# Attention output computed transposed and normalised straight from PSUM, in an attention and mixture-of-experts kernel

## What is computed

```python
c = einsum('bsi,bij->bsj', x, cond_weight[ids]) + cond_bias[ids][:, None, :]
Q, K, V = lora_linear(c, ...).reshape(B, 64, 16, 16)          # one each
scores = einsum('bqhd,bkhd->bhqk', Q, K) / 4 + slopes * (k - q)
attn = softmax(scores, axis=-1)
out = einsum('bhqk,bkhd->bqhd', attn, V).reshape(B, 64, 256)
out = lora_linear(out, Wo, bo, Ao, Bo)
x = x + (c + rezero * out)
```

## Time and profile before

| | |
|---|---|
| runs | 883.76, 883.92, 885.71 us, median 883.92 |
| profiled execution | 885.9 us, of which the span from first to last instruction is 884.0 |
| PE busy, PEld busy | 828.5 us (94%), 689.5 us (78%) |
| DVE, ACT, POOL busy | 543.3 us (61%), 294.2 us (33%), 402.7 us (46%) |
| mean granted clock of PE | 0.986 |

### The profile page before, as it was taken

One profiled execution on the slowest core, in us unless ns is written; L12 is line 12 of the kernel. 1 busy time (PEld: TensorE's weight loads), 2 busy tenths in 40 slices (PEclk: granted clock), 3 DMA queues, 4 the chain that ended last, 5 costly groups with the idle time before them and its releaser, 6 DMA issues.

```text
span 884.0 us, 28455 instructions
## 1 busy us (share of the span) xinstructions
PE 828.5 (94%) x9821; PEld 689.5 (78%) x9822; DVE 543.3 (61%) x1231; ACT 294.2 (33%) x783; POOL 402.7 (46%) x511
## 2 busy tenths in 40 slices
PE   6899999999999999979999799999999999999995
PEld 5777777777777778856777588888888888888884
DVE  3675565556555556758887356666666666666662
ACT  0233323333333333334323223343333333333330
POOL 2133343334334444210100357676777676767662
PEclk7999999999999999999999899999999999999998
DMA  8445555454454443104862313232323232323222
GB/s 274 139 118 153 163 163 161 143 147 147 151 159 134 140 149 106 46 1 138 250 231 71 118 25 37 35 37 32 36 33 37 32 37 32 37 31 37 32 35 24
DMA packets 49004, 85.60 MB, mean 97 GB/s; under 512 B 7266, under 2 KB 27554, under 8 KB 48834
## 3 DMA queue, kind: packets, MB, share of 16 engines
q1 hardware_dynamic: 33634, 68.76, 25.2%
q0 software_dynamic: 13888, 15.13, 13.2%
q10 hardware_dynamic: 1440, 1.16, 0.5%
HBM read 68.48 MB, written 16.55 MB: 96 GB/s over the span
## 4 chain that ended last, share of the span: by engine, by line
PE 76%; POOL 8%; issue 6%; DVE 5%; ACT 2%; ACTq 1%; DMA 1%; POOLq 1%; another core or an unknown queue 0%; DVEq 0%
PE ps L1409 22%; PE ps L1397 13%; PE ps L1310 6%; PE ps L1113 5%; PE ps L1392 4%; PE ps L1188 3%; PE ps L1299 3%; PE ps L1132 3%; PE ps L1380 2%; PE ps L1160 2%; PE ps L1172 2%; PE ps L1203 2%; PE ps L1100 2%; PE ps L1219 1%; POOL be_bc L407 1%
## 5 line engine op out<-in xcount | busy, mean ns | idle before, releaser
L1409 PE MATMUL ps<-arena,stage 128*128 x900 | 206.6, 379 | 0.0
L1409 PEld LDWEIGHTS ps<-arena,stage 128*128 128x128 f32 x900 | 165.2, 190 | 19.5
L476 POOL DMA_INDIRECT out_dram<-stage,to_row x75 | 120.6, 1608 | 89.8 <-DVE stage L1030 85.2
L634 ACT ACTIVATE stage<-ps 128x384 f32<-128x384 f32 x150 | 71.3, 490 | 232.6 <-PE ps L1397 229.8
L1397 PE MATMUL ps<-token_rows,token_rows_T 64*128 64x128 f32 x1800 | 144.6, 289 | 0.0
L1397 PEld LDWEIGHTS ps<-token_rows,token_rows_T 64*128 64x128 f32 x1800 | 120.7, 191 | 0.0
L468 POOL DMA_INDIRECT token_rows<-gated_rows,from_row x75 | 75.1, 1001 | 76.6 <-DVE to_row L918 54.0
L1008 DVE COPY token_rows<-ps 128x128 f32<-128x128 f32 x75 | 21.9, 291 | 131.1 <-PE ps L1381 131.1
L386 POOL TENSOR_TENSOR arena<-arena 128x256 f32<-128x256 f32 x32 | 23.3, 728 | 172.6 <-DVE arena L759 172.5
L1015 DVE TENSOR_TENSOR stage<-ps,stage 128x384 f32<-128x384 f32 x150 | 75.9, 546 | 2.0 <-ACT stage L634 2.0
L1113 PE MATMUL ps<-arena 128*128 128x128 f32 x512 | 67.4, 286 | 5.5 <-ACT arena L529 5.5
(11 more groups left out here) (170 smaller groups left out, 1482.6 us busy)
## 6 DMA issues: line engine op xcount, KB each, us to landing
stage<-in_we_dram SPq DMA_DIRECT2D x36, 512.0 KB, 4.3
arena<-in_cond_w_dram SPq DMA_DIRECT2D x64, 256.0 KB, 2.9
arena<-in_we_dram SPq DMA_DIRECT2D x12, 768.0 KB, 4.8
arena<-in_x_both_dram SPq DMA_DIRECT2D x32, 256.0 KB, 2.6
arena<-in_L_cond_bias_dram SPq DMA_DIRECT2D x64, 64.0 KB, 2.8
out_dram<-arena SPq DMA_DIRECT2D x32, 128.0 KB, 1.7
be_bc<-in_be_rows_dram SPq DMA_DIRECT2D x13, 192.0 KB, 2.8
gated_rows<-token_rows POOLq DMA_DIRECT2D x2, 1152.0 KB, 10.3
```

The costliest lines, as they stand in the source:

```text
L476: pool.indirect_dma_start(out_rows, bass.IndirectOffsetOnAxis(to_row[:, t:t + 1], 0), y_sb[t % YR], None, compute_op=ALU.add).then_inc(d_a ...
L634: nc.scalar.activation(g_sb[hf], ps[:, 2 + hf, 0:HH], ACT.Gelu).then_inc(g_ok, 1)
L1409: last = mm(ps[:, 4 + s % 2, 0:D], actT_sb[s % 2][:, hf, j * P:(j + 1) * P], arena[:, ds(e * E2 + (NJ * hf + j) * D, D)], start=(hf == 0 a ...
```

## The change

The output is computed transposed. The stationary operand is now `vD`, 128 partitions by 32 columns (V of two heads, block-diagonal, without the columns of ones), and the moving one is the block of `probsT`, 64 columns. The result has 32 features of two heads on the partitions and 64 queries in the columns; g selects the 32 partitions, m and b the columns, so that the 16 products fill columns 0 to 255 of bank 7 with the output in the layout that `oT` has. Beside each stands a second product with the constant `head_ones` (128x32, ones in the rows of a head for its 16 columns), which gives that head's row sums, repeated over its 16 partitions, in columns 256 to 511 of bank 7. `normalize` takes the reciprocal of all 256 columns of sums and multiplies, and its result is `oT` itself. `o_transpose` and `oT_copy` are gone, and so are the four DVE copies of ones into `vD` at the start. In `merge_b` the new `attend` runs between the two halves of the merge (after L1219, ahead of L1223); in steps without a merge it comes after `condition`, as the last work of the step. `score`, with its wait for `o_sb(i-1)`, is untouched.

```diff
-        vD = [cut(2, 8, 34) for _ in range(2)]
+        vD = [cut(2, 8, 2 * HD) for _ in range(2)]
...
-        onorm = cut(D)
+        inverse = cut(D)
...
-            def oT_copy(i):
-                act.wait_ge(oT_ps, i + 1)
-                copy(oT, ps[:, 7, 0:D].rearrange("p (c n) -> p c n", c=KC)).then_inc(oT_sb, 1)
...
-            for s in range(2):
-                for h in range(2):
-                    V.tensor_copy(vD[s][:, :, :, 32 + h],
-                                  col["kv"][:, h:h + 1].unsqueeze(2).to_broadcast([P, 2, 8]))
...
             def normalize(i):
                 dve.wait_ge(o_ps, i + 1)
-                V.reciprocal(rsum.rearrange("p (a h) -> p a h", h=2), o_acc[:, :, 32:34]).then_inc(rsum_sb, 1)
-                dve.wait_ge(rsum_sb, i + 1)
-                V.tensor_tensor(onorm.rearrange("p (a h d) -> p a h d", h=2, d=HD),
-                                o_acc[:, :, 0:32].rearrange("p a (h d) -> p a h d", h=2),
-                                rsum.rearrange("p (a h) -> p a h", h=2).unsqueeze(3).to_broadcast([P, 8, 2, HD]),
+                if not isinstance(i, int) or i > 0:
+                    dve.wait_ge(att_ps, i)
+                V.reciprocal(inverse, ps[:, 7, D:2 * D]).then_inc(inverse_sb, 1)
+                dve.wait_ge(inverse_sb, i + 1)
+                V.tensor_tensor(oT.rearrange("p c n -> p (c n)"), ps[:, 7, 0:D], inverse,
                                 ALU.mult).then_inc(o_sb, 1)
...
-                for g in range(4):
-                    for m in range(KC):
-                        hp = 4 * m + g
-                        for b in range(2):
-                            last = mm(ps[b * S:(b + 1) * S, 2, hp * 34:(hp + 1) * 34],
-                                      probsT[:, 2 * g + m, b * S:(b + 1) * S], vD[int(odd)][:, b, hp, :],
-                                      start=True, stop=True)
-                last.then_inc(o_ps, 1)
-
-            def o_transpose(i):
-                pe.wait_ge(o_sb, i + 1)
                 if not isinstance(i, int) or i > 0:
                     pe.wait_ge(x2T_sb, i)
-                for c in range(KC):
-                    last = tr(ps[:, 7, c * P:(c + 1) * P], onorm[:, c * P:(c + 1) * P], ident)
-                last.then_inc(oT_ps, 1)
+                for m in range(KC):
+                    for b in range(2):
+                        for g in range(4):
+                            r, at = slice(32 * g, 32 * g + 32), m * P + b * S
+                            p = probsT[:, 2 * g + m, b * S:(b + 1) * S]
+                            mm(ps[r, 7, at:at + S], vD[int(odd)][:, b, 4 * m + g, :], p, start=True, stop=True)
+                            last = mm(ps[r, 7, D + at:D + at + S], col["head_ones"], p, start=True, stop=True)
+                last.then_inc(o_ps, 1)
 
             def output(i):
-                pe.wait_ge(oT_sb, i + 1)
+                pe.wait_ge(o_sb, i + 1)
...
-            def merge(n, j, arrived, rows):
+            def merge(n, j, arrived, rows, inside=lambda: None):
...
                            stage_w[j][:, c, 2 * g:2 * g + 2, :], start=(c == 0), stop=(c == KC - 1))
+                inside()
...
-                if not isinstance(i, int) or i > 0:
-                    o_transpose(i - 1)
...
-                attend(i, odd)
                 if two_more:
                     condition(i + 2, odd)
                 if merge_b:
-                    merge(*merge_b, rows=i - 1 if late else None)
+                    merge(*merge_b, rows=i - 1 if late else None, inside=lambda: attend(i, odd))
+                else:
+                    attend(i, odd)
```

More of the change, by code:

```diff
@@ L34 @@
 NEG = -3.0e38
-CONST_COLS = dict(ident=P, tri=P, kmask=2, kv=2, count_down=NE, tile_start=NT, slot_tile=NS,
+CONST_COLS = dict(ident=P, tri=P, kmask=2, count_down=NE, tile_start=NT, slot_tile=NS,
                   block=NLANG * NE, past_high=1, past_mid=1, lang_row=1, one_row=1,
-                  in_tile=P, part_back=1, pad_row=1, id_high=2 * PAIRS, half=2)
+                  head_ones=2 * HD, in_tile=P, part_back=1, pad_row=1, id_high=2 * PAIRS, half=2)
 SMALL_COLS = dict(wr_raw=KC * NE, bq=KC, bk=KC, rz=1, wr=NE)
@@ L135, in adaln_attn_moe @@
         smax = cut(H)
-        rsum = cut(H)
         wm = [cut(KC, D) for _ in range(4)]
@@ L223, in adaln_attn_moe @@
         (c_ps, c_ok, cT_ps, cT_sb, xbo_sb, xres_sb, q_ps, q_sb, k_ps, v_ps, k_sb, v_sb, s_ps, max_sb, shift_sb,
-         prob_sb, pT_ps, pTa_sb, pTv_sb, o_ps, rsum_sb, o_sb, oT_ps, oT_sb, att_ps, x2_sb, x2T_ps, x2T_sb,
+         prob_sb, pT_ps, pTa_sb, pTv_sb, o_ps, inverse_sb, o_sb, att_ps, x2_sb, x2T_ps, x2T_sb,
          t_ps, t_sb, tT_ps, tT_sb, lg_sb, kept_t, kept_x2) = [sem(n) for n in (
              "c_ps c_ok cT_ps cT_sb xbo_sb xres_sb q_ps q_sb k_ps v_ps k_sb v_sb s_ps max_sb shift_sb "
-             "prob_sb pT_ps pTa_sb pTv_sb o_ps rsum_sb o_sb oT_ps oT_sb att_ps x2_sb x2T_ps x2T_sb "
+             "prob_sb pT_ps pTa_sb pTv_sb o_ps inverse_sb o_sb att_ps x2_sb x2T_ps x2T_sb "
              "t_ps t_sb tT_ps tT_sb lg_sb kept_t kept_x2").split()]
@@ L565, in tile_steps @@
                     cT_copy(i + 1)
-                if not isinstance(i, int) or i > 0:
-                    oT_copy(i - 1)
                 if merge_a:
@@ L602, in _ @@
                 unit_copy(u, u)
-            oT_copy(NT - 1)
             tT_copy(NT - 2)
@@ L740, in pT_copy @@
                 V.tensor_copy(probsT[:, 4:8, :].rearrange("p a n -> p (a n)"), ps[:, 1, :]).then_inc(pTv_sb, 1)
-            o_acc = ps[:, 2, 0:8 * 34].rearrange("p (a n) -> p a n", n=34)
             def normalize(i):
                 dve.wait_ge(o_ps, i + 1)
-                V.reciprocal(rsum.rearrange("p (a h) -> p a h", h=2), o_acc[:, :, 32:34]).then_inc(rsum_sb, 1)
-                dve.wait_ge(rsum_sb, i + 1)
-                V.tensor_tensor(onorm.rearrange("p (a h d) -> p a h d", h=2, d=HD),
-                                o_acc[:, :, 0:32].rearrange("p a (h d) -> p a h d", h=2),
-                                rsum.rearrange("p (a h) -> p a h", h=2).unsqueeze(3).to_broadcast([P, 8, 2, HD]),
+                if not isinstance(i, int) or i > 0:
[3 more added lines that the diff above has]
+                V.tensor_tensor(oT.rearrange("p c n -> p (c n)"), ps[:, 7, 0:D], inverse,
                                 ALU.mult).then_inc(o_sb, 1)
@@ L1316, in _ @@
             low_rank(NT - 2, n_merge)
-            o_transpose(NT - 1)
             hidden(0, 0, 0)
@@ L1445, in shape_constants @@
         "kmask": ((p[:, None] % 32) // HD == np.arange(2)[None, :]),
-        "kv": (p[:, None] // S == np.arange(2)[None, :]),
+        "head_ones": (p[:, None] // S == np.arange(2 * HD)[None, :] // HD),
         "count_down": np.broadcast_to(NE - np.arange(NE), (P, NE)),
```

## The result

The changed kernel takes 966.3 us (960.4 to 972.6) against 883.8: ratio 1.093, 95% interval 1.089 to 1.097. It is 82 us slower, where the prediction said 42. The profiled execution is one of 963.85 us, with a span of 962.0.

A forecast was written before the change was run, and what follows sets the result against it. PE, busy for 94% of the span, was taken as the bound. Waits at the scores and end terms, 29.0 + 2.4 + 9.0 + 1.5 + 0.7 - 0.4 = 42.2 us, on 884.0 gave 926 us; range 908 to 954.

The forecast's parts named there:

- The reciprocal: DVE's normalisation: the reciprocal grows from 16 to 256 elements per partition and takes 1.80 us.
- The products: PE's attention products: 64 records in place of 32, taken as 1.13 us, a change of 0.
- lower bound of 0.68: Attention products on PE: 0.68 us if only the shorter weight load counts.
- the second rival: Attention products on PE: halved weight loads give 0.68 us, returning 14.4 us over 32 tiles, so 912; chance 0.02.
- The wait: PE before the score, waiting for DVE's normalised output: 2.07 us in a step with a merge.
- the slack of POOL's chain: PE before L1203 in odd steps: 1.64 us of slack absorbs most of the score's wait, leaving 0.2 each.
- the prediction's signs: Expected in the profile: PE idle near 2.1 us before the score in every second step, L1203's odd-step wait nearly gone.
- Steps without a merge: Scores 1 and 28 to 30, without cover: 2.25 us more each, 9.0 in all; score 31: 1.54 more.
- The transposes: Two PE transposes per tile and ACT's copy removed: gain 0 in even steps, 0.22 us more slack in odd ones.
- the fourth rival: PE's clock falls to half behind new idle stretches: 941 in a few steps, 1060 throughout the attention phase; chance 0.12.
- The prediction's own sign of being wrong: Wrong if the reciprocal is under 1 us, PE shows no score wait, or the attention phase's clock leaves 1.0.

The follow-up runs named there:

- e1_fill: The changed kernel with 30 dummy products, whose result nobody reads, at the end of each step ahead of the next score: 932.0 us, ratio 1.053.
- e11_low: The kernel before, with low_rank(i-2) moved ahead of the projections in all steps without a merge_a: 881.8 us, ratio 0.9955.
- e12_fill_nologit: e1_fill with the four DVE operations of logit_consts replaced by filling their result with zeros: 926.1 us, ratio 1.046.
- e9_fill8: The changed kernel with 8 dummy products at the end of each step ahead of the next score: 950.8 us, ratio 1.075.
- e7_early: The changed kernel with its attention products at their old place, ahead of the conditional layer, the score's wait kept: 903.9 us, ratio 1.022.

## Why the prediction missed

The sign was right, and so was the wait that carries the forecast; the size was half of what came, and the time lies outside the range. The step that failed is the clock, which I kept out of the sum and, in its full extent, out of the range; a one-time term was missing besides.

- **The reciprocal.** Forecast 1.80 us, measured 1.757. The fixed part of other forms plus 6.3 ns an element from two short reciprocals gave 1.77, good to 1%; I had rounded it up. The eight cycles an element that I read out of the Trainium skill ("VectorE: DVE Perf Modes", the 8-slice pipeline) would have been 2.3; the trace does not agree.
- **The products.** Forecast 1.13 to 1.15, measured 1.17 (178.81 to about 179.98), all four column groups at work. The lower bound of 0.68, on which the second rival stood, was a miscount: half the present spacing of 0.029 for all 64 records, and 0.22 for the last one, is 1.15, so halved weight loads would have gained nothing.
- **The wait.** Forecast 2.07 in a step with a merge. At full clock (e1_fill) an even step takes 12.50 against 10.43 for steps 2 and 26 before: 2.07. A pair of steps takes 26.05 against 23.90, 2.15 more, for 2.27 forecast; the odd steps did have the slack of POOL's chain, and the idle time before L1203 is gone. PE's idle time of about 2 us stands before every score, not before every second one as the prediction's signs had it; once in each pair of steps it only takes the place of the wait before L1203. Steps without a merge: 11.63 against 9.32, 2.31 for 2.25; the last one 10.81 against 9.31, 1.50 for 1.54.
- **The transposes.** Worth nothing, as forecast: PE's idle time before the projections became 0.46 us, and e11_low confirms what stood there.
- **A term left out.** The one-time work on DVE behind step 2, 6 us with the clock stretch behind it (932.0 - 926.1). I had said of the score's wait what stands behind it on PE, and of DVE only `c_add`; the work between the steps wasn't in my list.
- **The clock, the step that failed.** It was the fourth rival, with 0.12, half of that for a few steps (941) and half throughout the phase (1060). It came throughout the phase, in part of the steps: 34 us (966.3 - 932.0), and the range did not reach it. The prediction's own sign of being wrong, a clock in the attention phase that leaves 1.0, is what the profile shows. The rows that I had were a fall after 0.41 us of work in 3.9 and none after 1.74 in 3.5, and the new stretches lay between; I put them on the safe side without a reason. I also priced it as all or nothing. The price for each us at half speed was right: 3.8 in 10.2 is 0.37, and 34 us in about 89 are 0.38. What was wrong is how much of the phase runs at half speed: not none and not all of it, but falls of mostly 3.4 us, one or two in a pair of steps.

With the clock held up and the one-time work gone, e12_fill_nologit is 40.9 us above the kernel before in its session, where the other terms sum to 42.2. That its time of 926.1 meets the forecast of 926 so closely is chance: the two start from kernels before that differ by 1.

The clock also explains the spread of the changed kernel, 12 us, which e1_fill does not have. The mean clocks of its four runs, 0.946, 0.943, 0.936 and 0.934, stand in the order of their times, 960.4, 963.9, 968.8 and 972.6. From the first to the last the time at half speed grows from 104 to 128 us (2 x 0.054 x 958.5 and 2 x 0.066 x 970.7), and half of that difference is 12 us.

## What to carry to other kernels

An instruction saved inside a wait is worth nothing, and one lengthened inside a chain is paid in every step: before moving work from PE to a serial chain on another engine, list what covers that chain and what uses the same cover. When a forecast contains new idle stretches of PE of the size seen here (1.4 to 2.0 us) in every step, put the clock into the sum and its full price into the range, not among the rivals. A wait that the data no longer needs is worth taking out, but look for the next one behind it first.

## What the hardware showed that I had not expected

- The clock falls with far shorter idle stretches than the kernel before had shown, and for shorter times: 3.4 us at half speed behind 1.98 us idle, and even where 1.42 and 0.46 us of idle time stood 1.2 us apart (e9_fill8), while single stretches of 1.45 to 1.49 left it at 1.0 in eleven odd steps and the pair of 1.43 and 0.46 did so three times (e7_early).
- Thirty dummy products in each wait, whose result nobody reads, make the changed kernel 34 us faster.
- Where the attention products, with 32 columns of weights, stand between dense groups with 64 (e7_early), the step is 0.35 us longer, with no idle mark in the trace; that the change of width is the cause is inferred.
- DVE's reciprocal from PSUM takes 1757 ns for 256 elements per partition and 258 for 16: 6.2 ns for each further element, six times the 1.04 ns of other forms.
